# A recommendation tower's dense layers: samples on the partitions against features on the partitions, two tiles at a time

## The chip, the cores and the metric

One NeuronCore of a Trainium2 chip runs the whole kernel. The metric is the device time of one execution in microseconds (us); less is better. Three runs of the kernel before were timed, and one more execution was profiled.

## The reference

512 samples, each with a dense vector of 128 numbers and 26 table indices. Everything is float32.

```python
e = stack([tbl_0[ids[:, 0]], ..., tbl_25[ids[:, 25]]], axis=1)    # 512 x 26 x 128
combined = concatenate([dense[:, None, :], e], axis=1)            # 512 x 27 x 128
z = einsum('bfd,bgd->bfg', combined, combined)[:, iu, ju]         # 351 pairs
h = concatenate([z, dense], axis=1)                               # 512 x 479
h = maximum(h @ W_top1 + b_top1, 0.0)                             # 512 x 512
h = maximum(h @ W_top2 + b_top2, 0.0)                             # 512 x 256
y = h @ W_top3                                                    # 512 x 1
```

## The kernel before, in words

**Layout.** The samples are four tiles `t` of 128 (T = 4). In each, the 27 vectors of a sample are brought into the tile `feats`, a matmul of each sample's 27 vectors with themselves (a *gram*) gives the pair products, and two dense layers follow. Where precision matters, a float32 number is split into a high and a low part of type float32r, and a product is three matmuls: high by high, high by low, low by high.

**Selection (PE lines L344, L352, L369).** Twelve small tables are not gathered: each is loaded whole into `stage` (SyncE's DMA queue, four buffers), split by ACT (`make_hi`, L611) and DVE (`make_lo`, L785), and multiplied with a one-hot matrix of the indices. DVE makes seven of a step's eight one-hot chunks (`make_onehots`, L798), ACT the eighth (L629, L636). There are six steps of two tables. A step has 32 matmuls of 512 columns. The one-hot chunks have a single buffer: DVE writes chunk c of step n+1 once PE has used chunk c of step n. In the first step (`select_first`) PE takes each chunk of table 0's high part as it comes, and spreads the indices over the partitions with `spread_ids` (L329) ahead of the step and in the middle of it. Ahead of all this stand eight idle transposes of the identity (`warm_up`, L317).

**Gathers (POOL, L308).** The other 14 tables are gathered by indirect DMA, one DMA for each tile and table, 56 in all, in the order of the tiles. `rows` has two buffers, so the gathers of tile 2 wait for the transposes of tile 0, in groups of four tables (`transpose_group`, PE L389; ACT or DVE copies the result into `feats`, L661 and L807).

**Pairs.** `gram(t, h)`, h = 0 to 3 (PE L407, 32 products, each two instructions): ACT takes one half of its result (`copy_picked`, L668), DVE the rest by a predicated copy (L815). After four grams DVE's block transpose `order_by_sample` (L825), PE's `move_picked` (four transposes, L415), ACT's `split_hi` (L674) and DVE's `split_lo` (L832) turn the pairs into stationary operands with the samples as columns. Grams have three PSUM banks, so a gram waits for the DVE copy of the third gram before it.

**Layers.** Layer 1 of a tile has the samples on the output's partitions: 15 matmuls of 512 columns into one bank, with a 128x128 block of pairs (or of the dense vector) as stationary operand and w1 as the moving one (L419 to L421, L438, L439, L444). ACT's `relu1` (L693) writes h1, PE transposes it back in four pieces (`transpose_hidden`, L453), ACT and DVE split it (L653, L842), and layer 2 is a bias matmul (L465: two rows of `ones` by two rows of b2) and 12 matmuls of 256 columns (L470, L471, L477). DVE's `finish` (L852) multiplies max(h2, 0) with w3 and sums along the row into column t of `y`. At the end PE turns `y` (L575), DVE copies it (L921) and SyncE stores it (L292). The last tile's layer 1 runs in two halves of 256 columns (L498 to L515).

**Order.** Each engine's program is a list written by hand. PE, for t = 1 to 3: gram, part of layer 1 of tile t-1, gram, part, gram, part, gram; then the transposes of tile t+1, `transpose_hidden(t-1)`, `move_picked(t)`, dense part of layer 1 of tile t, layer 2 of tile t-1. PE is thus never more than one tile ahead of its layers. The list `turns` gives each transpose its bank (3, 4 or 5 in turn). SyncE loads tables, then w1 in three pieces and w2 in one; ACT and DVE split these too (`make_hi(S + v)`, `make_lo(S + v)`, L605, L779 and for w2 L599, L772; S = 12), in the place of the dead one-hots, so after the last selection step.

Of the kernel before, what the change touches and what calls it, by code (L numbers as in the profile page):

```python
# [5 lines left out]
CHUNKS = 8  # L6
# [3 lines left out]
def dlrm_tower_kernel(nc, ids, ids_rows, dense, sel_tables, tables, second, w1, w2, b2, w3, out):  # L10
# [19 lines left out]
    C1 = H1 // P  # L30
    HH, CH = H1 // 2, C1 // 2
# [8 lines left out]
    WARM = 8  # L40
# [21 lines left out]
    groups = [(t, q) for t in (0, 1) for q in range(NG)]  # L62
    AFTER = [max(0, min(n - 1, NG)) for n in range(NSTEP + 1)]
    turns = groups + [moved(0)]
    for t in range(1, T - 1):
        turns += [(t + 1, 0), (t + 1, 1), (t - 1, None), (t + 1, 2), moved(t)] + [(t + 1, q) for q in range(3, NG)]
    turns += [(T - 2, None), moved(T - 1), (T - 1, 0, None), (T - 1, 1, None)]
# [32 lines left out]
    with ExitStack() as ctx:  # L100
# [33 lines left out]
        pairs_hi = [sb(f"pairs_hi{i}", [P, NK, P], f32r) for i in range(2)]  # L134

        ids_f = pairs_hi[0][0:S].rearrange("p k n -> p (k n)")
        pairs_lo = [sb(f"pairs_lo{i}", [P, NK, P], f32r) for i in range(2)]
# [5 lines left out]
        w3_bc = sb("w3_bc", [P, H2])  # L143

        b2_sb = sb("b2_sb", [2, H2])
        b2_hi = sb("b2_hi", [2, H2], f32r)
        b2_rows = sb("b2_rows", [2, H2], f32r)
        minus_lower = sb("minus_lower", [2, 1])
        ones = sb("ones", [2, P], f32r)

        h1 = [distance[:, i, :] for i in range(2)]
        h1T_hi = [tab_hi[i][:, 0:C1, :] for i in range(2)]
        h1T_lo = [tab_lo[i][:, 0:C1, :] for i in range(2)]
        h2w3 = stage[0][:, 0:H2]
        y = sb("y", [P, T])
        y_rows = h2w3[0:T, 0:P]
# [5 lines left out]

        banks = ctx.enter_context(nc.psum_tensor("banks", [P, 8, H1], f32))
        l1_ps, l2_ps = banks[:, 6, :], banks[:, 7, :]
        l2_last = banks[:, 2, :]
# [9 lines left out]

        def l1_half(e):
            return l1_ps[:, 0:HH] if e == 0 else banks[:, 1, 0:HH]
# [48 lines left out]
        bias_hi_ready = sem("bias_hi_ready")  # L226
        bias_ready = sem("bias_ready")
        lower_ready = sem("lower_ready")
        ones_ready = sem("ones_ready")
# [6 lines left out]
        pairs_lo_ready = sem("pairs_lo_ready")  # L236
        layer1_done = sem("layer1_done")
        h1_ready = sem("h1_ready")
        layer2_done = sem("layer2_done")
        h1T_hi_ready = sem("h1T_hi_ready")  # L240
        y_ready = sem("y_ready")
        y_turned = sem("y_turned")
        y_rows_ready = sem("y_rows_ready")
# [21 lines left out]
        def _(sp):  # L265
# [23 lines left out]
            sp.dma_start(b2_sb[:], b2[0, :].partition_broadcast(2)).then_inc(small_loaded, 16)  # L289
            sp.dma_start(w3_bc[:], w3[0, :].partition_broadcast(P)).then_inc(small_loaded, 16)  # L290
            sp.wait_ge(y_rows_ready, 1)
            sp.dma_start(out.rearrange("p t -> t p"), y_rows).then_inc(stored, 16)  # L292
            sp.wait_ge(stored, 16)
# [20 lines left out]
        def _(pe):  # L314
# [103 lines left out]
            def dense_products(t, acc, cols):  # L418
                nc.tensor.matmul(acc, dense_hi[:, t, :], w1_hi[:, 0, cols], start=True, stop=False)  # L419
                nc.tensor.matmul(acc, dense_hi[:, t, :], w1_lo[:, 0, cols], start=False, stop=False)  # L420
                nc.tensor.matmul(acc, dense_lo[:, t, :], w1_hi[:, 0, cols], start=False, stop=False)  # L421

            def layer1_dense(t):
                if t == 0:
                    pe.wait_ge(ids_copied, BY_DMA)
                    pe.wait_ge(dense_lo_ready, 1)
# [113 lines left out]
            for t in range(1, T):  # L540
# [7 lines left out]
                if t == T - 1:  # L548
                    break
# [433 lines left out]
```

## Time and profile before

| | us |
|---|---|
| median of three timed runs | 113.29 |
| lowest, highest | 112.92, 114.68 |
| the profiled execution, its own time | 114.23 |
| its span in the trace | 112.4 |

| engine | busy, us | share of the span |
|---|---|---|
| PE (matmul) | 102.7 | 91% |
| PEld (weight load, overlaps PE) | 79.6 | 71% |
| DVE | 66.8 | 59% |
| POOL | 61.0 | 54% |
| ACT | 56.9 | 51% |

The span runs from the first instruction to the end of the last; 1.8 us of the execution's own time lie around it. All times in the rows are us from the start of the span unless ns is written. PE is TensorE, DVE VectorE, ACT ScalarE, POOL GpSimd, SP SyncE; a q behind the name is the engine's issuing side, and L12 is line 12 of the kernel. A row of a timeline says: start, duration, engine, line, operation, output <- inputs, shapes, number of instructions, and in brackets how long the engine had idled and what released it. Matmuls overlap: a matmul of 512 columns is recorded with some 0.39 us, while the next starts 0.23 us after it. In the chain of work the pieces do not overlap, so a PE piece there is the time by which PE moved on. "PEclk" is the granted TensorE clock, 1.00 for 2.4 GHz and 0.50 for 1.2 GHz.

### The profile page before, as it was taken

Reading aid. Unit: us, or ns where it says so; the run is one execution under the profiler, and the core shown is the slowest. Engines: PE = TensorE matmul, PEld = TensorE weight load, DVE = VectorE, ACT = ScalarE, POOL = GpSimd, SP = SyncE. Lnnn points to the kernel's source line nnn. Section 1 sums busy time; section 2 is a strip of 40 time slices with the busy share of each in tenths; the row PEclk is TensorE's granted clock in tenths of the full one; section 3 lists DMA queues with packets and bytes.
Section 4 is the critical chain, followed back from the end, with each engine's and each line's share of the span. In section 5 each row is a group of like instructions: output and inputs, shape, how many; then the busy total and the mean of one; then the engine's idle time right before and its main releaser. Section 6 shows DMA issues by size and latency. Waiting matters only on the chain.

```text
span 112.4 us, 3333 instructions
## 1 busy us (share of the span) xinstructions
PE 102.7 (91%) x1447; PEld 79.6 (71%) x1447; DVE 66.8 (59%) x113; ACT 56.9 (51%) x83; POOL 61.0 (54%) x63
## 2 busy tenths in 40 slices
PE   4679999999999999999999839999999999988981
PEld 4235777788888888888887627786868786668860
DVE  1499846999999998996001976326331652252132
ACT  2596900894984956998028427047014701152210
POOL 2787877777777777778777767777300000000000
PEclk9999999999999999999999985999999999999997
DMA  2999789999999995482121212222100000000000
GB/s 60 289 272 228 204 148 274 235 258 223 250 172 244 246 346 198 121 271 62 47 67 50 53 47 53 53 71 51 47 6 6 0 6 0 6 6 0 0 0 1
DMA packets 5885, 13.12 MB, mean 117 GB/s; under 512 B 1784, under 2 KB 2698, under 8 KB 5871
## 3 DMA queue, kind: packets, MB, share of 16 engines
q1 hardware_dynamic: 3018, 8.37, 27.1%
q0 software_dynamic: 1792, 3.67, 12.7%
q10 hardware_dynamic: 1060, 0.87, 5.4%
q8 instruction: 11, 0.18, 0.7%
q14 instruction: 4, 0.02, 0.1%
HBM read 12.89 MB, written 0.01 MB: 115 GB/s over the span
## 4 chain that ended last, share of the span: by engine, by line
PE 90%; DVE 4%; ACT 2%; issue 2%; POOL 0%; DVEq 0%; POOLq 0%
PE banks L369 33%; PE banks L407 11%; PE banks L352 6%; PE banks L389 6%; PE banks L344 4%; PE banks L438 4%; PE banks L444 3%; PE banks L439 3%; PE banks L329 3%; PE banks L470 3%; PE banks L415 2%; PE banks L317 2%; PE banks L471 2%; PE banks L477 1%; DVE ids_bc L825 1%
## 5 line engine op out<-in xcount | busy, mean ns | idle before, releaser
L308 POOL DMA_INDIRECT rows<-in_tbl,ids_sb x56 | 60.3, 1076 | 18.2 <-issue 16.1
L369 PE MATMUL banks<-onehots,tab_hi 125*128 125x512 f32 x80 | 31.6, 395 | 0.0
L369 PE MATMUL banks<-onehots,tab_lo 125*128 125x512 f32 x80 | 31.2, 390 | 0.0
L611 ACT ACTIVATE tab_hi<-stage 125x1024 fp32r<-125x1024 f32 (+1 forms) x12 | 11.9, 1016 | 11.6 <-PE banks L369 5.8
L369 PEld LDWEIGHTS banks<-onehots,tab_hi 125*128 125x128 f32 x80 | 15.0, 188 | 3.3 <-issue 0.4
L369 PEld LDWEIGHTS banks<-onehots,tab_lo 125*128 125x128 f32 x80 | 15.0, 188 | 3.0
L798 DVE TENSOR_SCALAR onehots<-ids_bc,row_of 125x1024 fp32r<-125x1024 f32 x21 | 14.3, 750 | 2.5 <-PE banks L352 2.4
L407 PEld LDWEIGHTS banks<-feats 128*27 128x27 f32 x1024 | 10.9, 106 | 6.3 <-DVE picked L815 3.3
L785 DVE TENSOR_TENSOR tab_lo<-stage,tab_hi 125x1024 fp32r<-125x1024 f32 x12 | 14.2, 1219 | 1.0 <-ACT tab_hi L611 1.0
L815 DVE COPY_PREDICATED picked<-second_of,banks 128x112 f32<-128x112 int32 x16 | 4.5, 281 | 16.8 <-ACT picked L668 16.8
L798 DVE TENSOR_SCALAR onehots<-ids_bc_h,row_of 125x1024 fp32r<-125x1024 int16 x21 | 14.4, 752 | 0.0
L407 PE MATMUL banks<-feats 128*27 128x27 f32 x1024 | 13.1, 194 | 0.8 <-issue 0.5
L668 ACT ACTIVATE picked<-banks 128x112 f32<-128x112 f32 x16 | 4.2, 263 | 18.5 <-PE banks L407 18.3
L644 ACT ACTIVATE feats<-banks 128x1024 f32<-128x1024 f32 x6 | 6.7, 1115 | 5.1 <-PE banks L369 5.1
L389 PE MATMUL banks<-ident,rows 128*128 128x128 f32 x56 | 8.6, 278 | 0.1
L779 DVE TENSOR_TENSOR onehots<-stage,onehots 128x1024 fp32r<-128x1024 f32 (+1 forms) x3 | 3.1, 1029 | 9.0 <-ACT onehots L605 9.0
L389 PEld LDWEIGHTS banks<-ident,rows 128*128 128x128 f32 x56 | 6.3, 141 | 1.8 <-issue 1.0
L661 ACT ACTIVATE feats<-banks 128x512 f32<-128x512 f32 (+1 forms) x10 | 6.5, 693 | 0.6 <-PE banks L389 0.6
L636 ACT ACTIVATE onehots<-distance 125x1024 fp32r<-125x1024 f32 x6 | 6.3, 1050 | 0.2 <-PE banks L369 0.2
L344 PE MATMUL banks<-onehots,tab_hi 125*128 125x512 f32 x8 | 4.8, 728 | 1.8 <-DVE onehots L798 1.8
L842 DVE TENSOR_TENSOR tab_lo<-banks,tab_hi 128x512 fp32r<-128x512 f32 (+1 forms) x5 | 2.9, 578 | 5.7 <-ACT tab_hi L653 5.7
L438 PE MATMUL banks<-onehots,pairs_hi 128*128 128x512 f32 x12 | 5.9, 491 | 0.0
(81 smaller groups left out, 131.6 us busy)
## 6 DMA issues: line engine op xcount, KB each, us to landing
stage<-in_tbl SPq DMA_DIRECT2D x11, 448.0 KB
stage<-in_w SPq DMA_DIRECT2D x3, 512.0 KB
rows<-in_tbl,ids_sb POOLq DMA_INDIRECT x56, 6.0
ids_bc_h<-ids_short_rows ACTq DMA_DIRECT2D x6, 128.0 KB, 6.6
stage<-in_tbl SPq DMA_DIRECT2D x11, 52.0 KB
stage<-in_tbl SPq DMA_DIRECT2D x2, 224.0 KB
dense_sb<-in_dense SPq DMA_DIRECT2D x1, 256.0 KB, 11.7
stage<-in_w SPq DMA_DIRECT2D x1, 256.0 KB
```

The source lines that it names most:

```text
L308: nc.gpsimd.indirect_dma_start(out=rows[:, t % RB, m, :], out_offset=None, in_=tables[m], in_offset=bass.IndirectOffsetOnAxis(ap=ids_sb[:, ...
L344: nc.tensor.matmul(bank(0, 0), tab_part(0, 0)[:, c, :], onehots[0:RP, c, 0, :], start=(c == 0), stop=False)
L352: last = nc.tensor.matmul(bank(0, k), tab_part(k, part)[:, c, :], onehots[0:RP, c, k, :], start=(part == 0 and c == 0), stop=(part == 1 an ...
L369: last = nc.tensor.matmul(bank(n, k), tab_part(i, part)[:, c, :], onehots[0:RP, c, k, :], start=(c == 0 and part == 0), stop=(c == CHUNKS ...
L389: last = nc.tensor.transpose(tr_ps(n)[:, c, :], rows[:, t % RB, m, :], ident[:])
L407: last = nc.tensor.matmul(gram_ps(u)[SLOT * s:SLOT * s + F, i, 0:F], x, x, start=True, stop=True)
L438: nc.tensor.matmul(l1_ps, x, w1_hi[:, k, :], start=False, stop=False)
L611: nc.scalar.activation(tab_part(i, 0)[:, first:, :], src[:, first:, :], ACT.Copy).then_inc(hi_ready, 1)
L644: nc.scalar.activation(dst, src, ACT.Copy).then_inc(selected_copied, 1)
L661: nc.scalar.activation(dst, src, ACT.Copy).then_inc(turn_by_act, 1)
L785: nc.vector.tensor_tensor(tab_part(i, 1), src, tab_part(i, 0).bitcast(f32), ALU.subtract).then_inc(lo_ready, 1)
L798: nc.vector.tensor_scalar(onehot(n, c), ids_of(n)[0:RP], row_of[:, c:c + 1], None, ALU.is_equal).then_inc(onehot_by_dve, 1)
```

## The change

Layer 1 and layer 2 swap their operands: the weights are stationary and the samples of two tiles (256 columns) move, so that the output has features on the partitions and samples on the columns. It is then already the moving operand of the next layer. The bias of layer 2 and w3 lie on the partitions (one small transpose, `turn_small`, of four loaded rows); the bias is added by the instruction that applies the relu; layer 3 is two float32 matmuls for each pair of tiles, with one column of w3 as stationary operand. The output is stored for each pair of tiles, from one partition. `gram(1, h)` comes ahead of all of layer 1, and the lists of PE, ACT and DVE are new from the first gram on. In the opening, `warm_up` has 6 transposes before `spread_ids(0)`, 6 behind it, and 2 behind each of the first seven matmuls of `select_first`.

```diff
-    WARM = 8
+    WARM = 6
+    FILL = 2
...
+        def l1_ps(n):
+            return banks[:, 6 + n % 2, 0:PN]
+        def l2_ps(m):
+            return banks[:, 1 + m, 0:PN]
...
                     nc.tensor.matmul(bank(0, 0), tab_part(0, 0)[:, c, :], onehots[0:RP, c, 0, :], start=(c == 0),
                                      stop=False)
+                    if c < CHUNKS - 1:
+                        warm_up(FILL)
...
+            def layer1(p, m):
+                n = C1 * p + m
+                cols = slice(P * m, P * (m + 1))
+                pe.wait_ge(pairs_hi_ready, PT * (p + 1))
...
+                    x = pairs_hi[:, k - 1, :, :]
+                    nc.tensor.matmul(l1_ps(n), w1_hi[:, k, cols], x, start=False, stop=False)
+                    nc.tensor.matmul(l1_ps(n), w1_lo[:, k, cols], x, start=False, stop=False)
...
+                    last = nc.tensor.matmul(l1_ps(n), w1_hi[:, k, cols], pairs_lo[:, k - 1, :, :], start=False,
                                             stop=(k == NK))
...
+            def layer2(p, c):
...
+                for m in range(C2):
+                    cols = slice(P * m, P * (m + 1))
+                    nc.tensor.matmul(l2_ps(m), w2_hi[:, c, cols], hi, start=(c == 0), stop=False)
+                    nc.tensor.matmul(l2_ps(m), w2_lo[:, c, cols], hi, start=False, stop=False)
...
+            def layer3(p):
...
+                for c in range(C2):
+                    pe.wait_ge(h2T_by_act if c == 0 else h2T_by_dve, p + 1)
+                    last = nc.tensor.matmul(y_ps(p), b2w3[:, C2 + c:C2 + c + 1], h2T[p][:, c, :], start=(c == 0),
+                                            stop=(c == C2 - 1))
...
             warm_up(WARM)
             spread_ids(0)
+            warm_up(WARM)
...
             gram(0, 2)
-            layer1_dense(0)
             gram(0, 3)
+            gram(1, 0)
             move_picked(0)
...
+            gram(1, 1)
+            gram(1, 2)
+            gram(1, 3)
+            transpose_group(2, 0)
+            transpose_group(2, 1)
+            turn_small()
+            layer1_dense(0, 0)
+            move_picked(1)
+            transpose_group(2, 2)
+            transpose_group(2, 3)
+            layer1(0, 0)
+            layer1_dense(0, 1)
+            layer1(0, 1)
+            gram(2, 0)
+            layer1_dense(0, 2)
+            layer1(0, 2)
+            gram(2, 1)
+            gram(2, 2)
+            gram(2, 3)
+            layer1_dense(0, 3)
+            layer1(0, 3)
+            for q in range(NG):
+                transpose_group(3, q)
+            move_picked(2)
+            for h in range(U):
+                gram(3, h)
+            layer2(0, 0)
+            layer2(0, 1)
+            move_picked(3)
+            layer2(0, 2)
+            layer2(0, 3)
+            layer1_dense(1, 0)
+            layer1(1, 0)
+            layer3(0)
...
+            layer2(1, 2)
+            layer2(1, 3)
+            layer3(1)
```

At the places left out after `layer3(0)` the rest of layer 1 of the second pair alternates with `layer2(1, 0)` and `layer2(1, 1)`. ACT's and DVE's new lists, around the first grams:

```diff
             copy_picked(0, 2)
             copy_picked(0, 3)
             make_hi(S + 2)
+            copy_picked(1, 0)
             split_hi(0)
             for v in range(3, WV + 1):
                 make_hi(S + v)
...
             split_lo(0)
             for v in range(3, WV + 1):
                 make_lo(S + v)
...
+            for h in range(U):
+                copy_picked(1, h)
+            order_by_sample(1)
+            split_lo(1)
```

## Rows read from the trace of the kernel before

**Rows 1.** The page: engine totals.

```profile
PE 102.7 (91%) x1447; PEld 79.6 (71%) x1447; DVE 66.8 (59%) x113; ACT 56.9 (51%) x83; POOL 61.0 (54%) x63
```

**Rows 2.** Timeline of PE, 0 to 20 us.

```profile
1.52 1.97 PE L317 MATMUL banks<-ident 128*128 128x128 f32 x8 [1.52 <-POOL ident L299]
3.42 1.22 PE L329 MATMUL banks<-pairs_hi,ident_r 12*128 12x512 f32 x2
6.41 2.69 PE L344 MATMUL banks<-onehots,tab_hi 125*128 125x512 f32 x4 [1.77 <-DVE onehots L798]
...
12.05 3.61 PE L352 MATMUL banks<-onehots,tab_hi 125*128 125x512 f32 x8
15.46 3.90 PE L352 MATMUL banks<-onehots,tab_lo 125*128 125x512 f32 x16
```

**Rows 3.** Timelines of DVE and ACT, 2 to 22 us.

```profile
2.54 0.42 DVE L861 CAST pairs_hi<-feats 12x512 fp32r<-12x512 int32 x1 [0.66 <-DMA feats<-in_ids_rows]
...
5.51 4.74 DVE L798 TENSOR_SCALAR onehots<-ids_bc,row_of 125x1024 fp32r<-125x1024 f32 x7
...
17.88 4.75 DVE L798 TENSOR_SCALAR onehots<-ids_bc,row_of 125x1024 fp32r<-125x1024 f32 x7 [2.39 <-PE banks L352]
...
21.05 1.06 ACT L611 ACTIVATE tab_hi<-stage 125x1024 fp32r<-125x1024 f32 x1 [0.54 <-DMA stage<-in_tbl]
```

**Rows 4.** Windows: length, busy PE, PEld, DVE, ACT, POOL, PEclk, DMA share, GB/s.

```profile
2.80:42.00 39.20, 37.43 (x143) 28.07 (x142) 34.66 (x46) 26.53 (x29) 30.80 (x28) 1.00 0.99 242
...
64.85:66.60 1.75, 0.00 (x0) 0.00 (x0) 1.42 (x5) 0.78 (x2) 1.29 (x2) 1.00 0.13 37
66.84:70.26 3.42, 3.42 (x72) 2.40 (x70) 2.06 (x3) 2.18 (x5) 2.50 (x4) 0.50 0.18 46
86.70:89.20 2.50, 2.46 (x23) 2.08 (x21) 1.04 (x3) 2.04 (x4) 0.00 (x0) 1.00 0.00 0
```

**Rows 5.** The chain in order of time: start, us, what.

```profile
50.89 7.30 PE banks L369 x32
...
76.11 0.44 PE banks L453 x4
...
78.75 0.31 PE banks L465
79.06 0.32 PE banks L470
79.37 0.12 PE banks L471
...
80.67 0.67 PE banks L407 x51
81.34 0.43 PE banks L438
81.77 0.24 PE banks L439
```

**Rows 6.** Timeline of DVE, 65 to 71 us.

```profile
65.45 0.28 DVE L815 COPY_PREDICATED picked<-second_of,banks 128x112 f32<-128x112 int32 x1 [0.20 <-ACT picked L668]
65.87 0.71 DVE L825 STREAM_TRANSPOSE ids_bc<-picked 128x512 f32<-128x512 f32 x1
...
69.21 1.23 DVE L772 TENSOR_TENSOR w_lo<-stage,w_hi 128x1024 fp32r<-128x1024 f32 x1 [0.25 <-ACT w_hi L599]
```

**Rows 7.** POOL's last gather, and time to landing of those after 60 us.

```profile
79.05 0.94 POOL L308 DMA_INDIRECT rows<-in_tbl,ids_sb  x1 [0.30 <-issue]
...
DMA to landing us min/median/max: 2.5/2.5/2.6
```

**Rows 8.** Timelines of PE and DVE, the last waits and the tail.

```profile
101.61 0.39 PE L498 MATMUL banks<-onehots,pairs_hi 128*128 128x256 f32 x1 [0.69 <-ACT pairs_hi L674]
...
110.00 0.38 PE L575 MATMUL banks<-ident,y 128*4 128x128 f32 x2 [0.59 <-DVE stage L852]
...
110.42 0.37 DVE L921 COPY stage<-banks 4x128 f32<-4x128 f32 x1 [0.47 <-PE banks L575]
```

More of the change, by code:

```diff
@@ L60, in moved @@
         return (t, "moved", None)
[L62 removed]
     AFTER = [max(0, min(n - 1, NG)) for n in range(NSTEP + 1)]
[L64 to L67, printed above, removed]
+    turns = [(t, q) for t in (0, 1) for q in range(NG)] + [moved(0), (2, 0), (2, 1), moved(1)]
+    turns += [(2, q) for q in range(2, NG)] + [(3, q) for q in range(NG)] + [moved(2), moved(3)]
     def turns_after(n):
@@ L142, in dlrm_tower_kernel @@
         w2_lo = sb("w2_lo", [P, C1, H2], f32r)
[L143 to L156, printed above, removed]
+        b2w3_rows = sb("b2w3_rows", [2 * C2, P])
+        b2w3 = sb("b2w3", [P, 2 * C2])
+        h1T_hi = [tab_hi[i][:].rearrange("p c n -> p (c n)").rearrange("p (c n) -> p c n", n=PN) for i in range(NP)]
+        h1T_lo = [tab_lo[i][:].rearrange("p c n -> p (c n)").rearrange("p (c n) -> p c n", n=PN) for i in range(NP)]
+        h2T = [distance[:, i, :].rearrange("p (c n) -> p c n", n=PN) for i in range(NP)]
+        y_row = sb("y_row", [1, BP])
         second_sb = sb("second_sb", [P, Q, NK], i32)
@@ L416, in move_picked, with turn_small, layer1_dense @@
                 last.then_inc(transposed, 1)
[L418 to L424, printed above, removed]
+            def turn_small():
+                pe.wait_ge(small_loaded, 32)
+                pe.wait_ge(ids_copied, BY_DMA)
+                nc.tensor.transpose(banks[:, 7, 0:2 * C2], b2w3_rows[:], ident[0:2 * C2, 0:2 * C2]).then_inc(
+                    rows_turned, 1)
+            def layer1_dense(p, m):
+                n = C1 * p + m
+                if n == 0:
                     pe.wait_ge(ids_copied, BY_DMA)
@@ L441, in layer1_lo @@
-            def layer1_lo(t):
-                pe.wait_ge(turn_by_dve, dve_turns(turns.index(moved(t)) + 1))
+                elif n == 1:
+                    pe.wait_ge(b2w3_ready, 1)
+                else:
+                    pe.wait_ge(h1T_lo_ready, n - 1)
+                cols, tiles = slice(P * m, P * (m + 1)), slice(PT * p, PT * (p + 1))
+                hi, lo = dense_hi[:, tiles, :], dense_lo[:, tiles, :]
+                nc.tensor.matmul(l1_ps(n), w1_hi[:, 0, cols], hi, start=True, stop=False)
@@ L473, in layer2_lo @@
-            def layer2_lo(t, acc, pieces=range(C1)):
-                n = turns.index((t, None) if t < T - 1 else (t, 0 if pieces[0] == 0 else 1, None))
-                pe.wait_ge(turn_by_dve, dve_turns(n + 1))
-                for c in pieces:
-                    last = nc.tensor.matmul(acc, h1T_lo[t % 2][:, c, :], w2_hi[:, c, :], start=False,
-                                            stop=(c == C1 - 1))
-                if pieces[-1] == C1 - 1:
-                    last.then_inc(layer2_done, 1)
```

348 lines of the change are left out of this document (135 added, 213 removed).

## The prediction

> **What bounds the kernel now.** I read the engine totals first: TensorE (PE) is busy for 91% of the span, nobody else for more than 59% [rows 1]. So what counts is work taken off PE and holes in PE. I then took PE's timeline for the opening, the windows with the granted clock, the chain in order of time, and last the other engines at the holes.
>
> Three stretches. (a) The first selection step, to 19.4 us, is slow: four matmuls of 512 columns take 2.69 us because each waits for a one-hot chunk (seven in 4.74 us, 0.68 each), and the eight behind them, with all chunks there, take 3.61 us, 0.45 each. From about 15.5 the same shape takes 0.24 (16 in 3.90) [rows 2, 3]. 0.45 is the 1.2 GHz level and 0.24 the 2.4 GHz level; the granted clock that the page writes there is 1.00 all the same, so here I go by the durations. What PE did before the rise: it had idled 1.77 us at 4.6, then worked with holes, then without. (b) Selection steps 2 to 6, to 58.2 us, 7.3 us for each 32 matmuls, PE full [rows 5]. (c) From 58.2 to 112.4, 54.2 us: grams, transposes and layers. PE is nearly full there but for a hole of 1.8 us at 64.85, after which the granted clock was 0.50 for 3.4 us [rows 4], a hole of 0.69 and the tail [rows 8].
>
> **The opening.** Six transposes ahead of the first spread in place of eight: 8 took 1.97, so two less give back 0.49, and the indices are there (DVE's cast ends at 2.96) [rows 2, 3]. All of the one-hot chain moves up by that; its seventh chunk is ready at 9.8 in place of 10.25. The six transposes behind the spread (1.5 us) lie in the hole of 1.77 and cost nothing. The 14 fills: at 0.25 each they cost 0.49 a chunk, with the matmul 0.94, more than DVE's 0.68; at 0.12 they and the matmul take 0.48 and hide under DVE. So all hangs on whether the fills lift the clock. For it: for 2.5 us from 86.70 PE did 23 operations, nearly all transposes, and the granted clock stayed 1.00, while 1.75 us of nothing were followed by the fall [rows 4]. So transposes count as work. If the clock is up by about 8 us, PE ends the first chunk round at 10.6 in place of 12.25, and its 24 other matmuls take 5.5 us in place of 7.1: step 1 is done at 16.1, 3.3 us early.
>
> Is that passed on? DVE waited 2.39 us for PE at 17.88 [rows 3], so it moves up with PE, but then comes table 5: ACT waited for its landing at 21.05, and the DMA share is 0.99 from 2.8 to 42 us [rows 3, 4]. The load is issued only 0.5 us earlier (after `make_lo(1)`), so ACT's split, its copy of the indices and its one-hot (1.0 us each) hold PE at the last chunk of step 2: 24.7 to 25.2 against 27.5, a gain of 2.4 to 2.9. I take 2.6. Behind that, DVE's seven chunks (0.68 each) and two splits (1.2 each, as w2's [rows 6]) are 7.2 us a step, no more than PE's 7.3, so the gain lasts: selection ends at 58.2 - 2.6 = 55.6. Bounds: 3.3 gained; 1.6 lost if all 14 fills run at the slow level and the rise comes no sooner.
>
> *The Trainium skill (TensorE: Matmul & The Clock Gate, Part 4: PE-mode transpose) speaks against the fills: transposes do not count as busy for the clock gate in the way matmuls do. By it the opening would lose rather than gain; the window at 86.70 disagrees, as far as holding the clock goes. That transposes also raise it, no row shows. It is rival 1.*
>
> **The layers, as a balance of PE's time after the selection.**
> Columns: layer 1 streams 15 x 512 a tile before, 60 x 256 a pair after; layer 2 12 x 256 a tile before, 24 x 256 a pair after. Both equal. A matmul of 256 columns moves PE on by 0.12 and one of 512 by 0.23 to 0.24 [rows 5], so halving costs nothing, as long as the weight load stays hidden (rival 4).
> - Hidden transposes gone: 16 at 0.11 (4 in 0.44) [rows 5]: -1.8.
> - Bias matmuls gone: 0.31, and the next one takes 0.32 in place of 0.12 [rows 5]: 4 x 0.5 = -2.0.
> - Changes between float32 and float32r work: the first layer matmul after a gram takes 0.43 against 0.24 [rows 5], so 0.2 each time. Runs of layer matmuls: 18 before, 7 after: -2.2.
> - Added: `turn_small` 0.1; layer 3 of the first pair. No row has that shape; the nearest is L575, a float32 product, two instructions of 128 columns recorded in 0.38 with 0.27 for one, so 0.11 apart [rows 8]. 256 columns: 0.22 an instruction, 0.9 for two products; if it ran like float32r, 0.24. I take 0.9. Together +1.0.
> - Waits. Before: 1.8, 0.69 and some 0.4 of small ones. After: `gram(1, 0)` (0.67) fills part of the hole in front of `move_picked(0)`, but the dense matmuls (0.9) that kept the third bank's copy off the path are gone. Counted from the old times less 2.6: gram(0,3) ends 61.3, gram(1,0) 62.1; ACT and DVE copies (0.3 each), then the block transpose (0.71) [rows 6], ready 63.65: 1.6 us of hole. Then a new one: gram(1,3) needs DVE's `copy_picked(1, 0)`, and that is queued behind `split_lo(0)` and w2's `make_lo`, which waits for ACT's split of w2 and takes 1.23 [rows 6]. move_picked(0) ends 64.1, ACT splits pairs to 64.9 and w2 to 65.8, DVE w2 to 67.0, the copy to 67.2; grams (1,1) and (1,2) end at 65.5: 1.7 us of hole. Later 0.4 in front of `move_picked(2)`, whose bank ACT must free. 2.9 before, 3.7 after: +0.8.
> - Clock. Before, 3.42 us at 0.50 lost 1.7 [rows 4]. After, holes of 1.6 and 1.7 with 1.8 of work between: it may fall again, but part of the slow time would lie under the holes. Bounds 0 and 1.7; I take 0.3: -1.4.
> - Tail. Before, from the last layer matmul (109.4) to 112.4: 3.0. After: relu 0.4, the second product of layer 3 and its latency 0.9, the copy of 256 numbers on one partition 0.4 to 0.5 (128 took 0.37) [rows 8], issue and store 1.6 as before; with hand-overs 3.6: +0.6.
>
> Sum: -1.8 - 2.0 - 2.2 + 1.0 + 0.8 - 1.4 + 0.6 = -5.0.
>
> **The gathers.** POOL is a bound of its own: its last gather starts at 79.05 and lands 2.5 later, 81.6 [rows 7], and nothing in the change makes it earlier (56 in series). The changed PE wants that group after layer 1 of pair 0, by my replay at 82. So it just fits, and any greater gain ahead of it is lost. What follows the last group took 22 us in the replay, so the span does not fall below about 103.5.
>
> Together -2.6 - 5.0 = -7.6: span 112.4 to 104.8. The profiled execution, 114.23, would be 106.6; it is 0.94 above the median, 113.29, which would be **105.7**.
>
> **Rivals.**
> 1. *Fills do not lift the clock.* The chunk round then takes 7 x 0.94, the spread 1.15 and the last matmul 0.45 from 5.9 on: to 14.1 in place of 12.25. With the rise at 15.5 as before, three of the 24 other matmuls are slow and 21 fast: 20.4 against 19.4, and up to 1.6 late with a later rise. Selection ends some 1.2 later than before instead of 2.6 earlier: 105.7 + 3.8 = 109.5. For: the eight transposes and the spread of before did not raise it by 4.6 us. Against: the window at 86.70.
> 2. *The clock falls at the two new holes* and the slow time is not under them: +1.4: 107.1. For: 1.75 us idle did it before. Against: each hole is a bit shorter, with work between.
> 3. *Table loads hold the selection* more than table 5 did: DMA share 0.99, tables 8 to 11 wanted 2.6 us earlier. Gain 1.0 in place of 2.6: 107.3. Against: the wait for table 5 is the only one for a landing that the trace has among the tables.
> 4. *Slower: the weight load comes into the open.* The stationary operand is now a slice of w1 or w2. If the load (0.19 in the trace for the same 128 columns) were no longer hidden under 0.12 of streaming, 168 matmuls x 0.07 = 11.8: 117.5. It decides from 0.045 a matmul on. Against: the 256-column matmuls of layer 2 had the same load and moved PE on by 0.12.
>
> **Chances.** Forecast 0.60; rivals 0.12, 0.13, 0.12, 0.03. The range: below, the gathers' floor, 103.5 + 0.9 = 104.4, less a little for its own error: 103.6; above it takes in rivals 2 and 3, and most of 1: 109.0. Two per cent, about what a measurement of this kernel can tell from no change, is 111.0 and 115.6: faster 0.94, within 0.04, slower 0.02.
>
> **What would show it.** Matmuls of L344's kind at 0.24 before 9 us, DVE's second round of chunks at 14.6 to 15.4, the last selection matmul at about 55.6 (right); still 0.45 at 12 us (rival 1). ACT waiting for `stage` at later tables (rival 3). A hole of PE in front of the move of tile 0, and one in front of gram(1,3) released by DVE. Layer matmuls 0.12 apart (rival 4 wrong); layer 3 products 0.44 apart. PE close to the last gather at 82. Wrong I would be most in the holes: they are read from a replay of the lists by hand, and a wait that I overlooked in ACT's or DVE's new lists adds its whole length.

## The result, and the profile after

| | before | after |
|---|---|---|
| median of five runs, us | 114.13 | 119.11 |
| lowest, highest | 112.92, 115.19 | 117.57, 120.09 |
| ratio, 95% interval | | 1.044 [1.030, 1.059] |
| profiled execution, its span | 114.23, 112.4 | 119.11, 117.2 |

The kernel is 4.4% slower where I had forecast 7% faster. The span is 12.4 us above the forecast of 104.8. Below, lines carry the numbers of the kernel after: grams are L410, the selection L372 (its first step L345 and L355), transposes L392, `move_picked` L418, layer 1 L441 to L457, layer 2 L473 to L478, layer 3 L489.

The page, engine totals and the row of the granted clock (one digit for each fortieth of the span); it answers to [rows 1]:

```profile
PE 102.9 (88%) x1497; PEld 85.7 (73%) x1497; DVE 67.2 (57%) x109; ACT 55.9 (48%) x82; POOL 62.3 (53%) x63
...
PEclk9999999999999999999999555799999975599999
```

PE is as busy as before (102.9 against 102.7), although by the prediction's own terms the change takes some 5 us of work off it (1.8 + 2.0 + 2.2 - 1.0). Part of its time was at the low clock, and the holes grew from 9.7 to 14.3 us. The chain of work that ended last says whose they are: "issue" (PE waited for nothing that the profile shows) has 8% of it, against 2% before.

```profile
PE 79%; issue 8%; ACT 6%; DVE 4%; POOL 0%; DVEq 0%; POOLq 0%
```

**The opening.** PE's timeline, as [rows 2]:

```profile
3.00 1.21 PE L330 MATMUL banks<-pairs_hi,ident_r 12*128 12x512 f32 x2
...
6.97 0.78 PE L345 MATMUL banks<-onehots,tab_hi 125*128 125x512 f32 x1
7.54 0.63 PE L318 MATMUL banks<-ident 128*128 128x128 f32 x2
7.82 0.78 PE L345 MATMUL banks<-onehots,tab_hi 125*128 125x512 f32 x1
...
9.80 0.72 PE L330 MATMUL banks<-pairs_hi,ident_r 12*128 12x512 f32 x2
...
12.16 2.00 PE L355 MATMUL banks<-onehots,tab_hi 125*128 125x512 f32 x8
14.00 3.79 PE L355 MATMUL banks<-onehots,tab_lo 125*128 125x512 f32 x16
```

The first chunks come 0.85 us apart (6.97, 7.82): PE is at the 1.2 GHz level, and matmul and fills take longer than DVE's 0.68. At 9.80 the spread takes 0.72 in place of 1.21: the rise is between 9.3 and 9.8, where before it was at 15.5. The matmuls behind the chunk round begin at 12.16, no earlier than before (12.05), but the 24 of them take 5.6 us in place of 7.2. The selection ends at 56.6 in place of 58.2: 1.6 us gained.

**The grams.** PE's timeline from 60 us on:

```profile
62.92 1.61 PE L410 MATMUL banks<-feats 128*27 128x27 f32 x102 [1.21 <-issue]
65.23 1.11 PE L418 MATMUL banks<-ident,ids_bc 128*128 128x128 f32 x4 [0.69 <-DVE ids_bc L803]
66.27 2.23 PE L410 MATMUL banks<-feats 128*27 128x27 f32 x128
69.42 0.48 PE L410 MATMUL banks<-feats 128*27 128x27 f32 x21 [0.92 <-DVE picked L793]
70.97 0.77 PE L410 MATMUL banks<-feats 128*27 128x27 f32 x43 [1.07 <-issue]
...
85.75 0.27 PE L392 MATMUL banks<-ident,rows 128*128 128x128 f32 x1
86.43 1.87 PE L392 MATMUL banks<-ident,rows 128*128 128x128 f32 x13 [0.41 <-issue]
...
89.03 1.13 PE L410 MATMUL banks<-feats 128*27 128x27 f32 x108
92.32 1.31 PE L410 MATMUL banks<-feats 128*27 128x27 f32 x128 [2.16 <-issue]
96.05 0.49 PE L410 MATMUL banks<-feats 128*27 128x27 f32 x20 [2.41 <-issue]
```

The holes of 1.21, 1.07, 2.16 and 2.41 have "issue" behind them, no semaphore, and lie in the middle of a gram. The profile records a gram's 32 products as 64 matmuls, and beside each matmul stands a weight load, so a gram is 128 instructions. Between the last two holes there are exactly 128 matmuls, so 256 instructions; they take 1.31 us to run, and the next ones start 3.73 us after them. PE has the operands and the bank; what it lacks is instructions. The view of waits sums it for the grams at 6.9 us.

The trace shows the instructions on their way. The page has a DMA queue q8 of the kind "instruction"; its rows after, before, and in the experiment e11 below, which leaves 1024 of PE's instructions out:

```profile
q8 instruction: 12, 0.20, 0.7%
...
q8 instruction: 11, 0.18, 0.7%
...
q8 instruction: 7, 0.11, 0.4%
```

Its packets have 16,384 bytes each, and 1024 instructions less are four packets less: 256 instructions a packet. The packed trace holds the time of each packet. Beside the five holes named issue from 60 us on, in the kernel after:

| packet starts | packet has landed | PE goes on | after landing | hole |
|---|---|---|---|---|
| 60.22 | 61.55 | 62.92 | 1.37 | 1.21 |
| 68.50 | 69.45 | 70.97 | 1.52 | 1.07 |
| 83.94 | 85.01 | 86.43 | 1.42 | 0.41 |
| 89.91 | 90.78 | 92.32 | 1.54 | 2.16 |
| 93.35 | 94.70 | 96.05 | 1.35 | 2.41 |

Each hole ends 1.35 to 1.54 us after a packet has landed. The packets are not sent for far ahead: after PE has gone on, the next one starts 1.0 us (92.32 to 93.35) to 1.7 us (70.97 to 72.70) later, and once 3.5 us later (86.43 to 89.91), so that there 5.9 us lie between one block of instructions and the next. What those 3.5 us come from was not looked into.

**The clock.** Windows (columns as in [rows 4]):

```profile
64.70:75.30 10.60, 8.09 (x215) 6.97 (x216) 4.51 (x9) 4.05 (x10) 8.16 (x8) 0.53 0.20 53
95.40:102.20 6.80, 6.15 (x47) 6.09 (x47) 1.68 (x3) 0.86 (x2) 0.00 (x0) 0.52 0.01 2
```

It fell once before, for 3.4 us; now it was low for nearly all of two stretches of 10.6 and 6.8 us (means of 0.53 and 0.52), each time behind holes in the grams.

**Layers and tail.**

```profile
76.14 0.28 PE L454 MATMUL banks<-pairs_hi,onehots 128*128 128x256 f32 x1
76.26 0.28 PE L453 MATMUL banks<-pairs_hi,onehots 128*128 128x256 f32 x1
...
114.05 1.02 PE L489 MATMUL banks<-distance,b2w 128*1 128x256 f32 x4 [0.54 <-ACT distance L642]
115.11 0.59 DVE L828 COPY y_row<-banks 1x256 f32<-1x256 f32 x1 [1.08 <-PE banks L489]
```

Layer matmuls are 0.12 apart at the high clock. The layers do what they were priced at; the time is lost in the grams around them.

### The profile page after: what moved, and what is told of

Same layout as the page of the kernel before. It is cut to its first block, busy times and chain, and to the rows that moved or that the text cites. A ratio compares the mean times of both kernels' runs of the same rounds, so it can differ in the third digit from the quotient of the medians.

```text
span 117.2 us, 3415 instructions
## 1 busy us (share of the span) xinstructions
PE 102.9 (88%) x1497; PEld 85.7 (73%) x1497; DVE 67.2 (57%) x109; ACT 55.9 (48%) x82; POOL 62.3 (53%) x63
## 4 chain that ended last, share of the span: by engine, by line
PE 79%; issue 8%; ACT 6%; DVE 4%; POOL 0%; DVEq 0%; POOLq 0%
PE banks L372 31%; PE banks L410 7%; PE banks L355 5%; PE banks L392 4%; PE banks L453 3%; PE banks L318 3%; PE banks L457 3%; PE banks L454 3%; PE banks L345 3%; PE banks L418 3%; PE banks L473 3%; PE banks L474 2%; ACT feats L650 2%; PE banks L330 2%; PE banks L478 2%
## 5 line engine op out<-in xcount | busy, mean ns | idle before, releaser
L309 POOL DMA_INDIRECT rows<-in_tbl,ids_sb x56 | 61.5, 1099 | 18.1 <-issue 16.5
L372 PE MATMUL banks<-onehots,tab_hi 125*128 125x512 f32 x80 | 31.6, 395 | 0.0
L372 PE MATMUL banks<-onehots,tab_lo 125*128 125x512 f32 x80 | 31.2, 390 | 0.0
L410 PE MATMUL banks<-feats 128*27 128x27 f32 x1024 | 13.6, 200 | 8.4 <-issue 6.9
L410 PEld LDWEIGHTS banks<-feats 128*27 128x27 f32 x1024 | 11.6, 111 | 10.9 <-issue 8.3
L372 PEld LDWEIGHTS banks<-onehots,tab_hi 125*128 125x128 f32 x80 | 15.0, 188 | 3.3 <-issue 0.4
L372 PEld LDWEIGHTS banks<-onehots,tab_lo 125*128 125x128 f32 x80 | 15.0, 188 | 3.0
L657 ACT ACTIVATE picked<-banks 128x112 f32<-128x112 f32 x16 | 4.2, 264 | 13.7 <-PE banks L410 13.6
L816 DVE SCALAR_TENSOR_TENSOR tab_lo<-banks,tab_hi 128x256 fp32r<-128x256 f32 x8 | 3.4, 424 | 12.0 <-ACT tab_hi L638 12.0
L638 ACT ACTIVATE tab_hi<-banks 128x256 fp32r<-128x256 f32 x8 | 3.1, 384 | 14.6 <-PE banks L457 14.6
L392 PE MATMUL banks<-ident,rows 128*128 128x128 f32 x56 | 9.2, 298 | 0.4 <-issue 0.4
L392 PEld LDWEIGHTS banks<-ident,rows 128*128 128x128 f32 x56 | 7.1, 153 | 1.7 <-issue 0.9
L318 PE MATMUL banks<-ident 128*128 128x128 f32 x26 | 6.7, 390 | 1.5 <-POOL ident L300 1.5
L453 PE MATMUL banks<-pairs_hi,onehots 128*128 128x256 f32 x32 | 8.0, 282 | 0.0
L454 PE MATMUL banks<-pairs_hi,onehots 128*128 128x256 f32 x32 | 7.9, 279 | 0.0
```

The source lines that it names most:

```text
L309: nc.gpsimd.indirect_dma_start(out=rows[:, t % RB, m, :], out_offset=None, in_=tables[m], in_offset=bass.IndirectOffsetOnAxis(ap=ids_sb[:, ...
L318: nc.tensor.transpose(banks[:, 4, 0:P], ident[:], ident[:])
L372: last = nc.tensor.matmul(bank(n, k), tab_part(i, part)[:, c, :], onehots[0:RP, c, k, :], start=(c == 0 and part == 0), stop=(c == CHUNKS ...
L392: last = nc.tensor.transpose(tr_ps(n)[:, c, :], rows[:, t % RB, m, :], ident[:])
L410: last = nc.tensor.matmul(gram_ps(u)[SLOT * s:SLOT * s + F, i, 0:F], x, x, start=True, stop=True)
L453: nc.tensor.matmul(l1_ps(n), w1_hi[:, k, cols], x, start=False, stop=False)
```

## The experiments

The theory after this profile (A in the expectations): PE's instructions arrive in blocks of 256, about 3.7 us apart where nothing else holds PE; a gram uses 128 of them in 0.67 us, so in a long unbroken run of grams PE runs out of them and stands still, and behind that the clock falls. The kernel before puts a piece of layer 1 between any two grams of tiles 1 to 3. Rivals: the new opening costs something later, or the swapped layers themselves cost it.

To read the numbers: in all runs up to e11 the kernel before took 138 to 141 us (medians), not 114, with the same durations of single instructions at the high clock (a matmul of 512 columns 0.39, a gather 1.09 on average against 1.08), so the absolute times in the expectations do not apply, and each run is read against the kernel before beside it; e12 to e14 came back at 114. The time of a run is the median of its executions; where the text says that there is no ratio, the executions scattered too much for one.

### The two halves of the change, and the grams alone

e1 is the kernel after with the old opening, e2 the kernel before with the new one:

```diff
-    WARM = 6
-    FILL = 2
+    WARM = 8
+    FILL = 0
...
             spread_ids(0)
-            warm_up(WARM)
```

> The changed kernel with the opening of before (8 idle transposes, none between the chunks). If the opening's part is a gain of its own, as the trace of after shows it (selection ends 1.56 us earlier), this one ends its selection at 58.2 and takes 1.5 us more than the changed kernel, 6.5 more than before. If the opening does harm further on (its additional instructions, or another phase of the clock), this one is no slower than the changed kernel: 119 or less.

> The kernel before with the new opening alone, the layers untouched. If the opening's gain is passed on to the end: selection ends at 56.6 and the time is 1.5 us under before (ratio 0.987). If table loads or the gathers hold what follows: no gain in the end, ratio 1.00.

e3 is the kernel before with the four grams of each of tiles 1 to 3 in one run, all of layer 1 of the tile before behind them:

```diff
-                gram(t, 0)
-                layer1_hi(...)
-                gram(t, 1)
...
+                for h in range(U):
+                    gram(t, h)
+                layer1_hi(...)
+                layer1_lo(...)
```

> The kernel before with one thing changed: the four grams of tiles 1, 2 and 3 run one behind the other, and the layer matmuls that stood between them follow. Same work. Theory A, supply of instructions: a gram is 128 instructions in 0.67 us, and the trace of after shows 256 instructions for 3.7 us when four grams stand together, so gaps that nobody's semaphore ends appear inside the grams, 1 to 2.5 us a tile, and a fall of the clock behind them: 3 to 8 us slower, 117 to 122. Theory B, the gaps of after are waits for the copies by ACT and DVE or belong to the new layers: here the copies follow each gram within 0.6 us, so at most 0.5 us a tile, under 1.5 in all, and no gap of the kind called issue over 0.5 us.

e4 is the kernel after with half of the products of tile 3's grams left out:

```diff
-                for i in range(HB):
+                for i in range(0, HB, 2 if t == T - 1 else 1):
```

> The changed kernel with half of the products of tile 3's four grams left out (64 instructions a gram in place of 128); waits, order and all other work as they are. Theory A (supply of instructions): the two gaps of 2.16 and 2.41 us go, with them the slow clock from 95.4 to 102.2 (3.4 us lost) and 1.3 us of products: 6 to 9 us less than the changed kernel, 110 to 113. Theory B (waits): only the 1.3 us of products go and the gaps stay: 117 to 118.

| run | us | ratio to before |
|---|---|---|
| before | 139.59 | |
| e1 | 141.95 | 1.029 [1.011, 1.046] |
| e2 | 140.11 | 1.016 [1.002, 1.031] |
| e3 | 146.20 | 1.061 [1.051, 1.072] |
| e4 | 134.45 | 0.971 [0.957, 0.986] |

With the old opening the kernel is still slower, so the opening is not what makes it slow. Putting the grams together, with neither swapped layers nor new opening, costs 6%. In e3's timeline of PE the same holes stand where no gather runs any more (the last one starts at 85.61), with one of 1.91 at 110.04:

```profile
119.37 1.22 PE L407 MATMUL banks<-feats 128*27 128x27 f32 x119
121.97 1.31 PE L407 MATMUL banks<-feats 128*27 128x27 f32 x128 [1.39 <-issue]
125.42 0.26 PE L407 MATMUL banks<-feats 128*27 128x27 f32 x9 [2.14 <-issue]
```

e4 took 128 recorded matmuls, some 1.3 us, away, and is 7.5 us below e1, of which the opening explains at most 1.7. Of the two large holes in tile 3's grams one is gone, as one block of 256 instructions is, and one of 1.61 us is left; theory A had both gone. e2 came out slower than before, which no expectation had. These three were repeated, as e2b, e3b and e4b:

> The kernel of e2_new_opening once more (the kernel before with the new opening alone), since both chips so far took about 138 us for the kernel before. On a chip that takes 113 to 115 for it: 1.5 us less (ratio 0.987) if the opening's gain is passed on to the end, ratio 1.00 if not. On a chip that takes 138: no more than 1.5 us either way, hidden in the scatter.

> The kernel of e3_grams_together once more, since the chip of the first call took 139.6 us for the kernel before, with gaps called issue all over the grams. On a chip that takes 113 to 115: theory A says 3 to 8 us slower than before with gaps called issue inside the grams (ratio 1.03 to 1.07), theory B under 1.5 us (1.01).

> The kernel of e4_half_grams once more (half of the products of tile 3's grams left out). On a chip that takes 113 to 115 for the kernel before: theory A says 110 to 113 (ratio 0.96 to 0.99), the two gaps of over 2 us gone; theory B 117 to 118 (1.03).

e2b took 139.88 against 140.89, with no ratio: on the kernel before I can't say what the new opening does. In e2's trace it did its work (the 24 matmuls end at 17.9 in place of 19.3). e3b took 147.24 against 138.2, with no ratio, but its lowest execution (143.76) lies above the highest of before (140.84); e4b took 134.46, ratio 0.977 [0.971, 0.984]: both repeat.

### Grams spaced out in the kernel after

e5 alternates layer 1 of the first pair with the grams of tile 2, and layer 2 with those of tile 3; layer 2 of pair 0 gets two banks of its own for it, and ACT's and DVE's lists follow. e6 adds that w2 is split after the copies of tile 1's grams, so that `gram(1, 3)` does not wait for it.

```diff
             layer1(0, 1)
             gram(2, 0)
             layer1_dense(0, 2)
             layer1(0, 2)
             gram(2, 1)
-            gram(2, 2)
-            gram(2, 3)
             layer1_dense(0, 3)
             layer1(0, 3)
+            gram(2, 2)
+            gram(2, 3)
...
-            move_picked(2)
-            for h in range(U):
-                gram(3, h)
+            gram(3, 0)
             layer2(0, 0)
+            move_picked(2)
+            gram(3, 1)
             layer2(0, 1)
-            move_picked(3)
+            gram(3, 2)
             layer2(0, 2)
+            gram(3, 3)
             layer2(0, 3)
+            move_picked(3)
```

> The changed kernel's layers and opening, with another order on PE: the grams of tile 2 stand one by one between the four pieces of layer 1 of the first pair, those of tile 3 one by one between the four pieces of layer 2 (whose sums lie in banks 5 and 7 for it). Theory A (supply of instructions): no gap of over 0.5 us called issue in the grams of tiles 2 and 3 on a chip like the first one, the slow clock behind them gone, and 4 to 7 us less than the changed kernel: a ratio to the kernel before of 0.99 to 1.01. Theory B (the swapped layers themselves cost the time): the ratio stays at 1.04.

> e5_spaced, with the split of w2 (ACT 1.05 us, DVE 1.23 us) moved behind the copies of tile 1's grams. My first account put a hole of 1.7 us down to DVE's copy being queued behind that split. If that is what holds gram(1, 3): 1 to 1.5 us less than e5_spaced. If the supply of instructions holds these eight grams anyway (1024 instructions with only transposes between them, at 3.7 us for 256): no more than 0.4 us less.

e5: 137.83 against 138.2, no ratio. e6: 136.22, ratio 0.988 [0.979, 0.997]; whether splitting w2 later adds anything is not told, since e5's executions lie between 133.65 and 138.8. Then, with more runs, e6 again (e6b), e6 with the old opening (e9), and both kernels of the case:

> The kernel of e6_spaced_w2late again, on the same chip as the changed kernel: supply of instructions says 4 to 8 us less than the changed kernel (the gaps in the grams of tiles 2 and 3 gone or halved), the swapped layers being the cause says no difference.

> e6_spaced_w2late with the opening of before. If the opening's gain of 1.5 us is passed on, this takes 1.5 us more than e6; if the later work waits for instructions or gathers anyway, the same within 0.7 us.

> The kernel before, unchanged, for its trace on a chip of this kind (138 to 141 us so far in place of 113 to 115). If these chips supply instructions slower, the 24 us more lie in gaps called issue, in the grams above all, while matmuls, copies and transfers take what they took; if they are slower in other ways, durations of instructions or of transfers differ.

> The changed kernel, unchanged, on a chip of this kind, beside e6 and e9. Supply of instructions: its first eight grams, with only transposes between them, suffer more than those of before; ratio 1.03 to 1.05 as on the first chip. If the cost of the change were clock and waits alone: 1.02 or less here, where before has gaps too.

Before took 138.77; e6b 136.42, 0.983 [0.976, 0.990]; e9 138.14, 0.993 [0.985, 1.000]; the kernel after 143.27 (no ratio: its four executions lie between 138.09 and 145.77). With the same layers the order is thus worth 6.9 us between e8 and e6b by the medians and 3.8 by the lowest executions. In the traces the holes of 2.45 and 2.14 us in tile 3's grams of e8 are 0.80 and 0.57 in e6b. The opening is worth 1.7 us by the medians of e9 and e6b; the two intervals overlap, so this agrees with the 1.6 of the trace but does not show it.

### What makes these runs 24 us longer

e7, the kernel before once more (141.63), has this timeline of PE:

```profile
69.76 0.57 PE L407 MATMUL banks<-feats 128*27 128x27 f32 x45 [0.27 <-ACT feats L644]
70.58 0.26 PE L407 MATMUL banks<-feats 128*27 128x27 f32 x5 [0.25 <-issue]
71.30 0.27 PE L407 MATMUL banks<-feats 128*27 128x27 f32 x6 [0.46 <-issue]
...
89.12 0.29 PE L407 MATMUL banks<-feats 128*27 128x27 f32 x2 [0.40 <-issue]
...
90.91 0.97 PE L407 MATMUL banks<-feats 128*27 128x27 f32 x64
```

and POOL ends its gathers here:

```profile
88.33 1.76 POOL L308 DMA_INDIRECT rows<-in_tbl,ids_sb  x1 [0.30 <-issue]
```

PE gets some five matmuls (ten instructions) each 0.72 us, until about the end of the last gather; then a gram runs through again. That end of the trickle lies within 2 us of the end of the gathers in all six traces that I compared. This is another thing than the wait for a block: in e7 a packet of q8 has landed at 68.17 and the next one starts at 82.45, so for the first 12 us of the trickle none is under way. The trickle is not all of the 24 us either. The selection ends at 68.6 in e7 and at 58.2 before, and PE has holes named issue there from 42 us on. To see whether the gathers cause the trickle, or the sheer number of instructions: e10 is the kernel before without the 14 gathers of tile 3 (its grams take vectors already there; all of PE's work stays), e11 the kernel before with half of the products of all grams left out.

```diff
-            for t in range(T):
+            for t in range(T - 1):
...
-                pe.wait_ge(gathered[t][q], 16 * len(group(q)))
+                pe.wait_ge(gathered[t if t < T - 1 else 1][q], 16 * len(group(q)))
```

```diff
-                for i in range(HB):
+                for i in range(0, HB, 2):
```

> The kernel before without the 14 gathers of tile 3 (its transposes read the rows of tile 1, still in the buffer); PE, ACT and DVE do the same work. On the chips that take 138 us, the trickle of instructions (5 matmuls in 0.7 us) ended in all six runs within 1.3 us of POOL's last gather, at 86 to 90 us. Theory C, the gathers' transfers and the supply of instructions hinder each other: the trickle ends when the gathers do, near 70 us, and the time falls by 8 to 15 us, to 124 to 131. Theory D, the coincidence is one of time or of place in the program: the trickle goes on to 85 us or more, no more than 3 us gained. On a chip that takes 114: no gain over 1 us by either.

> The kernel before with half of the products of all 16 grams left out: 1024 of some 2900 PE instructions, 5.3 us of PE's time. Supply of instructions as the cause of the 24 us by which these chips are slower: the time falls by 15 us or more, to 123 or less. If the chips are slower for another reason (clock, waits, transfers): by 5 to 7 us, to 131 to 133.

Before took 138.7; e10 124.06, ratio 0.887 [0.877, 0.897]; e11 132.14, 0.955 [0.948, 0.963]. e10 is as expected: its last gather starts at 63.71, and the grams behind it run through:

```profile
70.32 0.74 PE L407 MATMUL banks<-feats 128*27 128x27 f32 x64 [0.27 <-ACT feats L644]
...
71.57 0.74 PE L407 MATMUL banks<-feats 128*27 128x27 f32 x64
```

What keeps e10 10 us above 114 stands ahead of the grams: its selection ends at 69.2, as late as in e7.

e11 missed the bound of 123 and met the other branch, 131 to 133. Half of the instructions of the grams were gone, yet the trickle went on to 83.8, near the end of the gathers (the last one starts at 85.50). So at this level it is the gathers, not the count of instructions, that hold PE in the grams. Why they do, no run shows.

### The deciding three

All three leave out tile 3's gathers, so that a trickle could not cover what was asked: e12 the kernel after, e13 the spaced kernel e6, e14 the kernel before (e10 again).

> The kernel after without the 14 gathers of tile 3 (its grams take tile 1's vectors as tile 0's rows are there; all of PE's work stays). e10 did the same to the kernel before: 124.06, without gaps in its first eight grams. Theory (long uninterrupted runs of grams outrun the supply of PE's instructions, whatever the gathers do): the first eight grams show gaps of 1 to 2.4 us, 256 instructions apart, the granted clock falls behind them, and the time is 1.03 to 1.06 of the kernel before with the same omission: 128 to 131. Rival (the gaps of the kernel after come from the gathers alone): without them its grams run at 0.74 to 0.95 for 64 instructions, and the layers' saving shows: 117 to 120.

> The spaced kernel (e6) with the same omission. Theory: layer matmuls of 256 columns between the grams let the supply catch up, so the gaps are mostly gone and the time is 117 to 121, against 128 to 131 for the kernel after. Rival (the swapped layers themselves cost the time): as the kernel after, within 1%.

> The kernel before with the same omission once more, on this chip, as the base of the two others: 122 to 126 by e10. Both theories expect the same here.

| run | us | ratio to before (complete, 114.26) |
|---|---|---|
| e12, grams as in the change | 117.61 | 1.036 [1.027, 1.045] |
| e13, grams spaced | 114.31 | 0.995 [0.989, 1.000] |
| e14, before | 113.86 | 0.996 [0.992, 1.000] |

The level was 114 this time, so the absolute times of e12, e13 and e14 (128 to 131, 117 to 121, 122 to 126) are missed by 10, 3 and 8 us; e12's falls into the 117 to 120 that its rival had named for the other level. In proportion, e12 stands at 117.61 / 113.86 = 1.033 to e14, inside the 1.03 to 1.06 of the theory, and not below it, as the rival has it; e13 is 3.3 us below e12 by the order alone. The rival by which the gathers alone make the gaps falls: e12 has them without tile 3's gathers. In its first eight grams they are 0.83, 0.59 and 1.03 us, smaller than the 1 to 2.4 expected.

```profile
61.57 1.11 PE L410 MATMUL banks<-feats 128*27 128x27 f32 x102 [0.83 <-issue]
...
65.33 1.36 PE L410 MATMUL banks<-feats 128*27 128x27 f32 x107 [0.59 <-issue]
...
69.06 0.76 PE L410 MATMUL banks<-feats 128*27 128x27 f32 x43 [1.03 <-issue]
...
87.38 1.13 PE L410 MATMUL banks<-feats 128*27 128x27 f32 x108
90.68 1.31 PE L410 MATMUL banks<-feats 128*27 128x27 f32 x128 [2.17 <-issue]
94.13 0.49 PE L410 MATMUL banks<-feats 128*27 128x27 f32 x20 [2.14 <-issue]
```

The same grams in e13:

```profile
91.70 0.40 PE L410 MATMUL banks<-feats 128*27 128x27 f32 x27 [0.80 <-issue]
...
92.60 0.39 PE L482 MATMUL banks<-tab_lo,w_hi 128*128 128x256 f32 x2
92.92 0.74 PE L410 MATMUL banks<-feats 128*27 128x27 f32 x64
...
94.49 0.37 PE L410 MATMUL banks<-feats 128*27 128x27 f32 x25
95.42 0.53 PE L410 MATMUL banks<-feats 128*27 128x27 f32 x39 [0.56 <-issue]
```

Count from hole to hole: 27 matmuls of a gram, 6 of layer 2, 64 of a gram, 6 of layer 2, 25 of a gram: 128 matmuls, 256 instructions, and 3.72 us apart. The period is that of the kernel after, but the layer matmuls fill it, so the holes are 0.80 and 0.56 in place of 2.17 and 2.14. With them goes the second fall of the clock; the windows of e12 and of e13:

```profile
95.00:100.00 5.00, 5.00 (x26) 5.00 (x26) 1.64 (x3) 0.60 (x1) 0.00 (x0) 0.52 0.02 3
```

```profile
95.00:100.00 5.00, 3.64 (x62) 3.19 (x62) 2.08 (x4) 1.23 (x3) 0.00 (x0) 1.00 0.02 3
```

In these 5 us e12 starts 26 matmuls and e13 62. Its first eight grams were not spaced (there is no layer work ready for them), and there the holes stand as in the kernel after:

```profile
62.89 1.11 PE L410 MATMUL banks<-feats 128*27 128x27 f32 x102 [1.36 <-issue]
...
66.66 1.53 PE L410 MATMUL banks<-feats 128*27 128x27 f32 x128 [0.77 <-issue]
70.66 0.76 PE L410 MATMUL banks<-feats 128*27 128x27 f32 x43 [2.47 <-issue]
```

The packets of q8 settle what the holes wait for. Behind the selection and outside the trickle, the 20 traces of this case hold 55 holes of PE named issue, of 0.18 to 2.47 us, in both kernels of the case and at both levels. Of these 54 end 1.26 to 1.56 us after a packet has landed, and one (0.31 us, in e2b) 2.17 after it.

The three above are 4.6 us of holes and the low clock from about 67 to 74, and so e13 only draws level with before. Taking all four grams of tile 1 ahead of layer 1 is built into working on two tiles at a time. At the 138 us level the spaced kernel (e6b) is 1.7% faster than the kernel before; at the 114 us level it was tried only without tile 3's gathers and is not told apart from before.

## Why the prediction was wrong, point by point

The step that failed is the term **Waits** (+0.8), and under it the way the balance was kept: PE's time was counted as durations of matmuls plus waits for semaphores, and the supply of instructions was taken as free. The holes that it makes came to 7.3 us (1.21 + 1.07 + 0.41 + 2.16 + 2.41), and with them the term **Clock** (-1.4) came out with the wrong sign. The rows for it were there: the trace of before had small holes named issue in grams, which I counted among the small waits without asking what they were.

```profile
64.47 0.37 PE L407 MATMUL banks<-feats 128*27 128x27 f32 x24 [0.29 <-issue]
...
80.60 0.74 PE L407 MATMUL banks<-feats 128*27 128x27 f32 x64
...
82.40 0.74 PE L407 MATMUL banks<-feats 128*27 128x27 f32 x64
...
94.88 0.30 PE L407 MATMUL banks<-feats 128*27 128x27 f32 x13 [0.20 <-issue]
```

The kernel before stood at that limit: from 80.60 to 82.40 a gram and four matmuls of 512 columns are 136 instructions in 1.8 us, so 256 in 3.4, a little less than the 3.7 of the blocks after.

Where the 12.4 us between forecast and span are:

- **Opening**: predicted -2.6, measured -1.6. The rise did come early, but past 9.3, not by 8; until then the fills held each chunk at 0.85 in place of 0.68. Rival 1 was wrong. All of the 1.6 was passed on, so rival 3 did not show. Difference: 1.0. Where the rise falls differs from one execution to the next: in e12, with the same opening, it came at 7.6, and the selection ended at 55.6, as forecast. The mechanism was right, and the size was partly a matter of the execution profiled.
- **First eight grams to the end of layer 1 of pair 0**: the replay said 82, PE was there at 85.75. Less the 1.0 of the opening, 2.7 us late. The issue holes here are 2.3; the wait of `gram(1, 3)` for DVE behind w2's split came as described, but took 0.9, not 1.7, and the one ahead of `move_picked(0)` 0.7, not 1.6, since PE itself was late. That leaves 2.1, which I put down to the clock without having summed it row by row.
- **From there to the end**: 22.8 predicted, 31.45 measured, 8.7 late. Issue holes 0.41 + 2.16 + 2.41 = 5.0. The 24 matmuls of layer 2 and `move_picked(3)` took 5.9 us at the low clock; by e13's rows (six in 0.79, the move 0.52) they are 3.7 at the high one: 2.2. The tail from the end of the last layer matmul (113.5) was 3.7, against 3.6 (the copy from one partition took 0.59, not 0.4 to 0.5). Some 1.4 is left, which I put down to a replay that was too short; it isn't traced further.

- **Clock** (-1.4): the sign was wrong. Rival 2 had one fall at two holes, at a cost of 1.4; there were two falls, and the low clock held for some 17 us in all.
- **Hidden transposes, bias, switches** (-6.0) and **layer 3** (+1.0): the durations that the rows show held. Layer matmuls were 0.12 apart, and the first pair's layer 3 took 0.95 against 0.9. That PE's busy time did not fall for all that, I put down to the low clock; the saving was not measured by itself. Rival 4 was wrong.
- **Gathers**: the last one was issued at 80.28 and wasn't waited for.

My slower case (0.02) was the weight load; the mechanism that decided was in no rival, though the 0.29 and 0.20 above were a reason to have one. The prediction's own warning, that an overlooked wait adds its whole length, named the right place, but a wait of ACT or DVE, not of PE's supply.

*The Trainium skill (Runtime: NRT & Kernel Launch, Instruction fetch mechanics) describes the store as a FIFO refilled in blocks of 256 instructions, and the cost of crossing a block as mostly hidden.* The count of 256 agrees with the rows of after, e12 and e13 and with the packets of q8; that the cost is hidden does not, wherever 256 instructions take less than about 3.7 us. By that page nothing would have been late; by the rows it is 7 us of 117.

That the holes are waits for instructions is shown by their place (each 256 instructions), by the packets of q8 that land 1.26 to 1.56 us before 54 of 55 of them end, and by the runs in which they shrink with what is put between the grams. What is not shown is why a packet is sent for no earlier.

## What to carry to other kernels

Beside the durations, count PE's instructions in each stretch (a float32 product of a gram is four, two matmuls and two weight loads, and cheap), and set them against the supply that the trace shows; here 256 in 3.7 us. Where short matmuls outrun it, put long ones between them, and treat an order that does so as part of the kernel's speed: a change that frees PE of work but bunches the short instructions can lose more than it frees. Holes called issue were such waits here down to 0.2 us: ask for their cause, by counting the instructions between two of them and by the packets of the instruction queue.

## What was not expected of the hardware

- A run of 27-column matmuls stalls every 256 instructions, with 3.45 to 4.0 us from one such start to the next (after 3.73, e12 3.45, e13 3.72 and 4.0), while 256 of them need 1.31 us. The steps of that period are in the trace: 1.0 to 1.7 us from where PE goes on until the next packet of instructions starts (3.0 to 4.0 in seven of 55 cases), 0.9 to 1.5 for the packet, and 1.26 to 1.56 until PE goes on.
- Idle transposes do help to raise the clock here. With 26 transposes of the identity in the opening in place of 8, and the same matmuls, the trace's first record of the granted clock lies between 7.6 and 10.3 us in all 11 traces that have them (after 9.83), and between 13.6 and 15.8 in the 9 that have the old opening (before 15.65). *The Trainium skill (TensorE: Matmul & The Clock Gate, Part 4: PE-mode transpose) says that they do not count like matmuls; this case's opening speaks against it.*
- The same kernel before took 113 to 116 us at some times and 137 to 145 at others. It is not the chip as such: one and the same chip gave 138.77 and, later, 114.26. In the long ones PE gets about ten instructions each 0.72 us in the grams while indirect gathers run, with no packet of instructions under way for most of that time. Removing a quarter of the gathers gave back 11% there, and 0.4% at the other level (e14). What sets the level stays open.
